# Nine of sixteen B products of a selective scan made by ScalarE on turned data and turned back by TensorE

## The reference

```python
xc = silu(conv(x @ in_w_x) + conv_b)            # 128 inner channels, T = 16384 tokens
dt, B, C = split(xc @ x_w.T)                    # 4, 16 and 16 wide
dt = softplus(dt @ dt_w.T + dt_b)
h_s[t] = exp(dt[t] * A_s) * h_s[t-1] + (dt[t] * xc[t]) * B_s[t]     # for 16 states s
y[t] = sum_s h_s[t] * C_s[t] + xc[t] * D
out = (y * silu(z)) @ out_w.T                   # and once more with time reversed
```

## Time and profile before

| | before |
|---|---|
| time, three runs | 2965.06 us median (2964.64 to 2966.75) |
| the profiled execution | 2967.89 us, span 2966.1 us |
| TensorE busy | 2497.7 us, 84% of the span |
| VectorE busy | 2318.3 us, 78% |
| GpSimd busy | 2084.2 us, 70% |
| ScalarE busy | 1576.8 us, 53% |
| mean granted TensorE clock | 0.90 of full |
| first scan forward to last scan backward | 851 to 2682 us |

### The profile page before, as it was taken

The page is one execution under the profiler, slowest core; times in us unless marked ns, Lnnn a source line. Parts: engine busy times, 40 slices in busy tenths (PEclk is TensorE's granted clock), DMA queues, the critical chain, the costliest instruction groups (busy, mean ns, idle before and its releaser), DMA issues. The chain is left out here.

```text
span 2966.1 us, 34800 instructions
## 1 busy us (share of the span) xinstructions
PE 2497.7 (84%) x7800; PEld 1190.2 (40%) x7800; DVE 2318.3 (78%) x2487; ACT 1576.8 (53%) x2784; POOL 2084.2 (70%) x1166
## 2 busy tenths in 40 slices
PE   7899999957468988889889858899889889988598
PEld 7666666624322323323323223333333333336422
DVE  4366666560659999999999939998999899895499
ACT  6466666543655655555656446555555555545221
POOL 3133333230359999999999949999999999995155
PEclk6699999969779999999999889999999999997599
DMA  3000000000256777777777637776766676660022
GB/s 60 8 9 9 9 9 9 6 1 0 59 167 223 243 244 237 247 235 240 246 236 241 227 124 235 219 236 216 229 226 222 221 225 224 218 211 17 13 54 47
DMA packets 177295, 437.72 MB, mean 148 GB/s; under 512 B 65638, under 2 KB 70219, under 8 KB 177228
## 3 DMA queue, kind: packets, MB, share of 16 engines
q1 hardware_dynamic: 139340, 420.19, 44.5%
q10 hardware_dynamic: 37888, 16.79, 2.1%
HBM read 404.40 MB, written 24.12 MB: 144 GB/s over the span
## 5 line engine op out<-in xcount | busy, mean ns | idle before, releaser
L1443 POOL TENSOR_TENSOR sb_hc<-sb_h,sb_cc 128x1024 f32<-128x1024 f32 x256 | 599.7, 2360 | 61.8 <-PE sb_py L1232 56.2
L1443 POOL TENSOR_TENSOR sf_hc<-sf_h,sf_cc 128x1024 f32<-128x1024 f32 x256 | 595.8, 2347 | 11.5 <-DVE sf_h L1521 8.2
L1232 PE MATMUL sf_py<-sf_hc,ident 128*128 128x512 f32 x1024 | 533.1, 655 | 0.6 <-POOL sf_hc L1443 0.6
L1232 PE MATMUL sb_py<-sb_hc,ident 128*128 128x512 f32 x1024 | 519.5, 638 | 0.0
L572 POOL TENSOR_TENSOR ar_sc<-ar_sc,ar_mx 128x512 f32<-128x512 f32 x128 | 154.7, 1208 | 356.6 <-DVE ar_mx L513 356.6
L1521 DVE TENSOR_TENSOR_SCAN sf_h<-sf_dA,sf_state,sf_pu 128x1024 f32<-128x1024 f32 x160 | 375.4, 2346 | 19.1
L1521 DVE TENSOR_TENSOR_SCAN sb_h<-sb_dA,sb_state,sb_pu 128x1024 f32<-128x1024 f32 x160 | 375.2, 2345 | 17.1
L1232 PEld LDWEIGHTS sf_py<-sf_hc,ident 128*128 128x128 f32 x1024 | 197.0, 205 | 269.3 <-issue 239.8
L1232 PEld LDWEIGHTS sb_py<-sb_hc,ident 128*128 128x128 f32 x1024 | 187.3, 196 | 241.0 <-issue 232.0
L1501 DVE TENSOR_TENSOR sb_pu<-sb_pu,sb_dtx 128x1024 f32<-128x1024 f32 x160 | 193.9, 1212 | 52.7 <-PE sb_pu L1212 52.7
L1436 POOL TENSOR_TENSOR sb_dbx<-sb_dtx,sb_bb 128x1024 f32<-128x1024 f32 x96 | 226.5, 2359 | 3.3 <-DVE sb_dtx L1482 3.3
(11 more groups left out here) (294 smaller groups left out, 4594.6 us busy)
## 6 DMA issues: line engine op xcount, KB each, us to landing
sf_cc<-rows_scratch SPq DMA_DIRECT2D x256, 512.0 KB, 4.4
sb_cc<-rows_scratch SPq DMA_DIRECT2D x256, 512.0 KB, 4.4
sf_bb<-rows_scratch SPq DMA_DIRECT2D x96, 512.0 KB, 5.4
sb_bb<-rows_scratch SPq DMA_DIRECT2D x96, 512.0 KB, 5.4
sf_n<-n_scratch SPq DMA_DIRECT2D x32, 258.0 KB, 5.4
sb_n<-n_scratch SPq DMA_DIRECT2D x32, 258.0 KB, 5.3
y_scratch<-sf_yo SPq DMA_DIRECT2D x16, 512.0 KB, 6.1
sb_yf<-y_scratch SPq DMA_DIRECT2D x16, 512.0 KB, 5.1
```

Source lines behind the costliest of these rows:

```text
L1232: ins = nc.tensor.matmul(p_y[:, hf], lhsT=c.ident[:, :], rhs=hc[:, s % RING, hf], start=False, stop=(s == U - 1))
L1443: nc.gpsimd.tensor_tensor(hc[:, s % RING, :], h[:, s % RING, :], cc[:, s % C_RING, :], ALU.mult).then_inc(read, 1)
```

## The change

`BY_V` shrinks from ten to four states and `BY_G` from six to three. The nine states of the new `BY_A` have their B product made with tokens on the partitions. For that, once per chunk, TensorE makes the B columns with tokens on the partitions (`columns_b`: eight products of 128 tokens x 16 states) and turns dt*x in eight blocks of 128x128 (`turn_x`); ScalarE copies both to SBUF (`take_columns_b`, `take_turned_x`). For each state of `BY_A`, ScalarE multiplies the eight blocks by the state's B column, which is a per-partition scale of an activation (`scale`, three units ahead, ring `sT` of two), and TensorE turns the eight blocks back into `p_u[s % 2]` (`turn_in`, one unit ahead, where `spread_b` stood). The decays of all thirteen states of `BY_V` and `BY_A` (`BY_D`) go to the ring `dA`.

State columns are kept two at a time: in units with odd s, at the end of the unit, the pair (s-3, s-2). The scan of an even state s waits for the pair (s-4, s-3), which is copied in ScalarE's unit s-1. The ring `bb` becomes one buffer, `store_parts` moves from unit 11 to 12 and `load_parts` from 12 to 14. State 0 is now one of GpSimd's.

```diff
-C_RING, B_RING, DECAY_RING = 4, 3, 5
-DECAY_AHEAD, INJECT_AHEAD, LAG_SUM = 3, 2, 4
-BY_G = (2, 5, 7, 10, 13, 15)
-BY_V = tuple(s for s in range(16) if s not in BY_G)
+C_RING, B_RING, DECAY_RING, TURN_RING = 4, 3, 5, 2
+DECAY_AHEAD, INJECT_AHEAD, SCALE_AHEAD, LAG_SUM = 3, 2, 3, 4
+BY_V = (1, 5, 8, 14)
+BY_A = (2, 3, 4, 7, 9, 10, 12, 13, 15)
+BY_D = tuple(sorted(BY_V + BY_A))
+BY_G = tuple(s for s in range(STATES) if s not in BY_D)
...
-        bb, dbx = sb("bb", [128, B_RING, TC]), sb("dbx", [128, B_RING, TC])
+        bb, dbx = sb("bb", [128, TC]), sb("dbx", [128, B_RING, TC])
...
+            def columns_b(m, par):
+                pe.wait_ge(r_copied, m + 1)
+                for j in range(BLOCKS):
+                    ins = nc.tensor.matmul(p_p[:, j * STATES:(j + 1) * STATES], lhsT=xc[:, par, j * Q:(j + 1) * Q],
+                                           rhs=k["bc"][:, 0:STATES], start=True, stop=True)
+                ins.then_inc(bt_made, 1)
+            def turn_x(m, par):
+                pe.wait_ge(dtx_done, m + 1)
+                for j in range(BLOCKS):
+                    ins = nc.tensor.transpose(p_p[:, j * Q:(j + 1) * Q], dtx[:, par, j * Q:(j + 1) * Q], c.ident[:, :])
+                ins.then_inc(x_turned, 1)
+            def turn_in(n, par, s):
+                r = BY_A.index(s)
+                pe.wait_ge(scaled, n * NA + r + 1)
+                need(pe, scanned, n * U + s - 1)
+                for j in range(BLOCKS):
+                    ins = nc.tensor.transpose(p_u[s % 2][:, j * Q:(j + 1) * Q], sT[:, (par * NA + r) % TURN_RING, j, :], c.ident[:, :])
+                ins.then_inc(turned_in, 1)
...
             def project(m, par, last):
                 pe.wait_ge(y_gated, m + 1)
-                pe.wait_ge(dt_done, NC if last else m + 3)
-                pe.wait_ge(dtx_done, NC if last else m + 3)
+                pe.wait_ge(xt_taken, NC if last else m + 3)
...
             prepare = [(0, convolve(a)), (0, convolve(b)), (2, in_out(a)), (3, in_out(b)),
-                       (5, step_size(a)), (6, step_size(b))]
+                       (4, columns_b), (6, step_size(a)), (6, step_size(b)), (13, turn_x)]
             if back:
-                run(pe, unit, prepare, [(13, project)], [(4, gate_in(a)), (4, gate_in(b))])
+                run(pe, unit, prepare, [(14, project)], [(5, gate_in(a)), (5, gate_in(b))])
...
+            def scale(n, par, s):
+                r = BY_A.index(s)
+                if r == 0:
+                    act.wait_ge(bt_taken, n + 1)
+                    act.wait_ge(xt_taken, n + 1)
+                need(act, turned_in, n * NA + r + 1 - TURN_RING)
+                for j in range(BLOCKS):
+                    ins = nc.scalar.activation(sT[:, (par * NA + r) % TURN_RING, j, :], dtxT[:, j, :], ACT.Copy,
+                                               scale=bT[:, par, j, s:s + 1])
+                ins.then_inc(scaled, 1)
...
             def keep(n, s):
-                act.wait_ge(scanned, n * U + s + 1)
+                act.wait_ge(scanned, n * U + s + 2)
                 e = 0 if back else TC - 1
-                nc.scalar.copy(state[:, s:s + 1], h[:, s % RING, e:e + 1]).then_inc(kept, 1)
+                nc.scalar.copy(state[:, s:s + 2], h[:, s % RING:s % RING + 2, e]).then_inc(kept, 1)
...
                 m, mpar, ms = after(n, par, s + DECAY_AHEAD)
-                if ms in BY_V and not (last and s + DECAY_AHEAD >= U):
+                if ms in BY_D and not (last and s + DECAY_AHEAD >= U):
                     decay_v(m, mpar, ms)
-                if s >= 2:
-                    keep(n, s - 2)
-                elif not first:
-                    keep(n - 1, s - 2 + U)
+                m, mpar, ms = after(n, par, s + SCALE_AHEAD)
+                if ms in BY_A and not (last and s + SCALE_AHEAD >= U):
+                    scale(m, mpar, ms)
+                if s % 2 and s >= 3:
+                    keep(n, s - 3)
+                elif s % 2 and not first:
+                    keep(n - 1, s - 3 + U)
...
-            prepare = [(1, silu_x), (4, bc_rows), (5, load_flat), (6, part_high), (7, softplus_relu), (7, softplus_abs),
-                       (8, softplus_exp), (8, softplus_one), (8, softplus_log), (9, part_middle), (11, store_parts),
-                       (11, take_dt), (12, load_parts)]
+            prepare = [(1, silu_x), (4, bc_rows), (5, load_flat), (5, take_columns_b), (6, part_high), (7, softplus_relu),
+                       (7, softplus_abs), (8, softplus_exp), (8, softplus_one), (8, softplus_log), (9, part_middle),
+                       (11, take_dt), (12, store_parts), (14, take_turned_x), (14, load_parts)]
...
-                run(act, unit, prepare, [(1, silu_z)], [(1, exp_log_tables), (5, take_z)])
+                run(act, unit, prepare, [(1, silu_z)], [(1, exp_log_tables), (6, take_z)])
...
-                need(dve, kept, u + 1 - RING)
+                if s % 2 == 0:
+                    need(dve, kept, n * PAIRS + (s - RING) // 2 + 1)
...
-                [(LAG_SUM - 1, gate), (14, add_x)] if back else [])
+                [(LAG_SUM - 1, gate), (15, add_x)] if back else [])
...
-                need(sp, g_injected, n * NG_ + r + 1 - B_RING)
-                spread_row(bb[:, r % B_RING, :], n, s, b_spread[r % B_RING])
+                need(sp, g_injected, n * NG_ + r)
+                spread_row(bb[:, :], n, s, b_spread)
```

More of the change, by code:

```diff
@@ L939 @@
 FLAT = STATES * TC // 128
+BLOCKS = TC // Q
 def state_space_stage(nc, c, W, y_scratch, rows, nd, split):
@@ L1072, in scan_direction @@
     U = STATES
-    NV, NG_ = len(BY_V), len(BY_G)
+    NV, NG_, NA, ND = len(BY_V), len(BY_G), len(BY_A), len(BY_D)
+    PAIRS = U // 2
     with ExitStack() as ctx:
@@ L1092, in scan_direction @@
         yo = sb("yo", [128, TC])
+        bT, dtxT = sb("bT", [128, 2, BLOCKS, STATES]), sb("dtxT", [128, BLOCKS, INNER])
+        sT = sb("sT", [128, TURN_RING, BLOCKS, INNER])
         if back:
@@ L1111, in scan_direction @@
             sem(s) for s in ("r_copied", "r_stored", "f_loaded", "high", "remained", "middle", "lowest", "p_stored"))
+        bt_made, bt_taken, x_turned, xt_taken, scaled, turned_in = (
+            sem(s) for s in ("bt_made", "bt_taken", "x_turned", "xt_taken", "scaled", "turned_in"))
         p_loaded = [sem("p_loaded%d" % j) for j in range(2)]
@@ L1114, in scan_direction @@
         c_spread = [sem("c_spread%d" % j) for j in range(C_RING)]
-        b_spread = [sem("b_spread%d" % j) for j in range(B_RING)]
+        b_spread = sem("b_spread")
         block = ctx.enter_context(nc.Block())
@@ L1127, in past @@
         def past(order, n, s, ring):
-            r = order.index(s) - ring
-            return n * U + order[r] + 1 if r >= 0 else (n - 1) * U + order[r + len(order)] + 1
+            r = order.index(s)
+            if r >= ring:
+                return n * U + order[r - ring] + 1
+            return (n - 1) * U + order[max(q for q in range(len(order)) if q % ring == r % ring)] + 1
         def run(eng, unit, prepare=(), tail=(), own=()):
@@ L1162, in step @@
                 def step(m, par, last):
-                    pe.wait_ge(r_copied, NC if last else m + 2)
+                    pe.wait_ge(bt_taken, NC if last else m + 2)
                     if last:
-                        pe.wait_ge(dt_done, NC)
-                        pe.wait_ge(dtx_done, NC)
+                        pe.wait_ge(xt_taken, NC)
                     ins = nc.tensor.matmul(p_p[:, hf], lhsT=k["z"][:, :],
@@ L1175, in step @@
                     pe.wait_ge(n_loaded[par], 16 * (m + 2 - par))
-                    need(pe, dt_done, m)
-                    need(pe, dtx_done, m)
+                    need(pe, xt_taken, m)
                     if back:
@@ L1189, in step @@
                 def step(m, par):
-                    pe.wait_ge(r_copied, m + 1)
+                    pe.wait_ge(bt_taken, m + 1)
                     if back:
@@ L1255, in unit @@
                     spread_b(m, mpar, ms)
+                if ms in BY_A and not (last and s == U - 1):
+                    turn_in(m, mpar, ms)
                 if s >= LAG_SUM:
@@ L1319, in take_dt @@
                 act.wait_ge(dt_summed, m + 1)
-                need(act, v_decayed, NV * (m - 1))
+                need(act, v_decayed, ND * (m - 1))
                 need(act, g_decayed, NG_ * (m - 1))
@@ L1329, in bc_rows, with take_columns_b, take_turned_x @@
                 nc.scalar.dma_start(rows[bass.ds(m, 1), :, :].rearrange("a r t -> (a r) t"), brow[:, :]).then_inc(r_stored, 16)
+            def take_columns_b(m, par):
+                act.wait_ge(bt_made, m + 1)
+                nc.scalar.copy(bT[:, par, :, :].rearrange("p j s -> p (j s)"), p_p[:, 0:BLOCKS * STATES]).then_inc(bt_taken, 1)
+            def take_turned_x(m, par):
+                act.wait_ge(x_turned, m + 1)
+                need(act, scaled, NA * m)
+                nc.scalar.copy(dtxT[:, :, :].rearrange("p j d -> p (j d)"), p_p[:, :]).then_inc(xt_taken, 1)
```

(29 more changed lines are left out.)

4 lines of the change are left out of this document (2 added, 2 removed).

## The result

The kernel with the change takes 3112.03 us median (3108.47 to 3118.13, four runs) against 2964.85 for the kernel before on the same chip: a ratio of 1.0505, 95% interval 1.0478 to 1.0532. Slower, as predicted, but by 147 us instead of 79. The profiled execution spans 3110.2 us against 2966.1 before, 144.1 more.

A forecast was written before the change was run, and what follows sets the result against it. Before, GpSimd bounds forward; with the change ScalarE was to set 59.0 us forward against 53.9 and 58.5 backward against 57.9. +76, +9, -6 each for last chunks, +3 each for first: +79 on 2966, 3045 us; range 2915 to 3160.

The forecast's parts named there:

- The scaling's price: ScalarE's 128x128 scalings by a B column pointer, 72 a chunk: 0.295 us each, 21.3 us a chunk.
- (1): Rival: ScalarE's scaling is cheap, 1.3 to 1.6 us a state; 2873 us, or up to 2900; chance 0.16.
- (3): Rival: a state's eight scalings on ScalarE don't overlap, 6.6 us more a chunk, 3250 us; chance 0.12.
- The four 512-column activations: Upper bound for the scaling on ScalarE: four take 2.37 us without overlap, so a scaling would be 0.39.
- ScalarE's sum: ScalarE's work per chunk adds up to 54.1 us before waits; over 50 us busy was the sign.
- the stall ahead of scan 0: VectorE loses 2.4 us, as state copies 12 and 13 come after 4.7 us and scan 15 covers 2.3.
- The DMA waits on ScalarE's path: Forward, ScalarE waits 1.0 us for the rows' store (landing 3.6) and 1.2 for the flat load (4.9).
- The rest of the forward sum: ScalarE's forward path from scan 14's end to keeping pair 8, 9: 48.9 us; with its tail 59.0.
- Which tail ends the chunk: Forward after pair 8, 9: VectorE's tail 9.4 us gives 58.3, ScalarE's 10.1 with the parts' store gives 59.0, taken.
- unit 4: TensorE's long backward unit, over 7 us, claimed hidden because scan 6 waits longer for ScalarE's pair 2, 3.
- rival (4): TensorE's clock falls to 0.85; backward 5 us more a chunk, 3120 us; chance 0.07.
- Rival (2): Waits vanish because ScalarE runs ahead elsewhere: 54.3 us forward, 55.2 backward, 2925 us; chance 0.12.

The follow-up runs named there:

- flat_later: The changed kernel with the flat load of the B rows and the first part issued later in ScalarE's program: 3069.8 us, ratio 1.0367 to before.
- half_turn: The changed kernel with only four of each state's eight blocks turned back, all eight still scaled (incomplete result): 3097.7 us, ratio 1.0458 to before.
- front_light: The changed kernel with single state copies and later flat load, minus seven of eight B column products and the backward D term: 3000.8 us, ratio 1.0138.
- six_thirteen: The changed kernel with six scaled states instead of nine, thirteen decays kept, single state copies and a later flat load: 3047.6 us, ratio 1.0284.
- both_half: The changed kernel with four of each state's eight blocks scaled and four turned back (incomplete result): 2968.4 us, ratio 1.0010 to before.

## Why the prediction was right or wrong

**The scaling's price: right.** 0.295 was taken, 0.304 measured. It was read from the exp with a pointer and lay between the copy's 0.16 and the full 0.39. Rivals (1) and (3) fall with it. The four 512-column activations that don't overlap were no guide for this form.

**ScalarE's sum and the stall ahead of scan 0: right.** It was to be over 50 us busy and is at 52.3 and 53.1. Before scan 0, VectorE was to lose 2.4 us:

```profile
1334.73 4.58 DVE L1586 TENSOR_TENSOR_SCAN sf_h<-sf_dA,sf_state,sf_pu 128x1024 f32<-128x1024 f32 x2
1342.01 2.35 DVE L1586 TENSOR_TENSOR_SCAN sf_h<-sf_pu,sf_state,sf_dbx 128x1024 f32<-128x1024 f32 x1 [2.70 <-ACT sf_state L1426]
```

It is 2.70 in this chunk (start, duration; in brackets the idle time and its releaser), and 39.7 us in 15 chunks. GpSimd at 0.78 of the chunk was foreseen too.

**The DMA waits on ScalarE's path: the term that was mis-sized.** Rows' store and flat load were put at 1.0 and 1.2 us. In a chunk of after, on ScalarE (ACTq is its queue issuing a DMA):

```profile
1360.67 0.98 ACT L1360 COPY sf_brow<-sf_pp 32x1024 f32<-32x1024 f32 x1
1361.82 0.36 ACTq L1362 DMA_DIRECT2D rows_scratch<-sf_brow  x1
...
1364.39 0.18 ACT L1426 COPY sf_state<-sf_h 128x2 f32<-128x2 f32 x1
1368.10 0.38 ACTq L1388 DMA_DIRECT2D sf_flat<-rows_scratch  x1
1368.53 0.27 ACT L1366 COPY sf_bT<-sf_pp 128x128 f32<-128x128 f32 x1 [3.96 <-DMA rows_scratch<-sf_brow]
```

ScalarE stands 3.96 us for the store, 3.2 in the mean. It has the size and the bytes of before, but lands later:

```profile
rows_scratch<-sf_brow ACTq DMA_DIRECT2D x16, 128.0 KB, 5.6
...
sf_flat<-rows_scratch ACTq DMA_DIRECT2D x16, 64.0 KB, 2.7
```

5.6 us against 3.6, and the flat load 2.7 against 4.9. I took a landing time of before as a constant. The store's wait costs 2.2 us a chunk more than I gave it, the flat load 1.0 less. The loads of the B rows, put at 5 us each at most, land 3.9 to 6.5 us after their issue forward, 4.8 in the median, but no product of GpSimd waits for one. flat_later shows that this wait is worth its full size forward: 3.2 us of it went and the period fell by 3.2.

**The rest of the forward sum.** Worked through the chunk whose zero (end of scan 14) is at 1337.05: the pairs are kept at 18.2 (0, 1), 27.3, 39.4, 48.2 and 53.9 us (8, 9); by the prediction's terms at 16.4, 24.5, 34.5, 43.2 and 48.9. So the path came out 5.0 us long in this chunk, of 63.7 in all. The mean chunk is 61.1, 2.1 over the 59.0 forecast: 2.2 - 1.0 from the two DMAs, 0.7 from the scalings (72 x 0.009), some 0.4 from single scalings that start 1.8 us late with no releaser in the trace (6.7 us in all of the direction), 0.75 from waits around y and its copy. The sum of these is 3.0, and as one tail fell away (next) they stand on a base of 58.3, so 61.3 of 61.1.

**Which tail ends the chunk: wrong.** I took ScalarE's, 59.0, because load_parts would wait for the store of the parts, 5.4 us. There is no such wait. The trace of ScalarE at the end of a chunk:

```profile
1389.94 1.14 ACT L1414 ACTIVATE sf_dA<-sf_dt,ss_A 128x1024 f32<-128x1024 f32 x1
1390.20 0.41 ACTq L1402 DMA_DIRECT2D split_scratch<-sf_parts  x1
...
1393.02 2.44 ACT L1380 ACTIVATE sf_sT<-sf_dtxT,sf_bT 128x128 f32<-128x128 f32 x8
...
1397.89 0.35 ACTq L1408 DMA_DIRECT2D sf_bcs<-split_scratch  x1
```

The store is issued at 1390.20, although in the program it stands behind the decay and the scaling that run from 1391.97 and 1393.02 to 1395.46. It lands in 1.9 us in the median, long before load_parts at 1397.89. Before, ScalarE did stand for this store, 47.4 us in 15 times; that wait was carried over. VectorE's tail is the one that counts, 9.4 predicted and 9.3 found. VectorE even sets the pace from scan 10 on: scan 10 waited for the pair 6, 7 in 15 chunks (45.4 us), scan 12 for the pair 8, 9 in one only. By the prediction's terms both ways round are equally long: 43.2 us for the pair 6, 7 and 15.25 for five scans and three passes of 1.2, 58.4 against 58.3. The right number then was 58.3 and not 59.0, by chance on the side that made my error smaller.

**Backward: the period near, the reason wrong.** 58.5 was forecast with ScalarE as its bound: scan 6 would wait for the pair 2, 3, and that would hide TensorE's unit 4. It is 60.2. Scan 6 never waited for a state copy there, and scan 7 waited for its turned block in every chunk, 3.9 us in the mean and in the row at 2077.36; before, VectorE had stood up to 3.4 us for a B row behind the same unit. So unit 4 was not hidden, and TensorE is on the path (half_turn, front_light). That the period came within 1.7 us is luck as far as its reason goes. In the trace of after:

```profile
2085.64 1.04 PE L1235 MATMUL sb_pu<-ident,sb_sT 128*128 128x128 f32 x8
2086.51 3.60 PE L1264 MATMUL sb_py<-sb_hc,ident 128*128 128x512 f32 x8
2092.37 1.19 PE L1235 MATMUL sb_pu<-ident,sb_sT 128*128 128x128 f32 x8 [2.26 <-DVE sb_h L1586]
2093.35 3.52 PE L1264 MATMUL sb_py<-sb_hc,ident 128*128 128x512 f32 x4
2096.71 1.04 PE L1235 MATMUL sb_pu<-ident,sb_sT 128*128 128x128 f32 x8
```

TensorE runs from 2042.17 with one gap of 0.73 to 2090.11, waits 2.26 us for a scan, and then the product of one state takes 3.52 for four instructions, where the eight of an earlier row took 3.60 and four take 1.88 one chunk later (below). The clock says why (stretches; granted clock is third from the end):

```profile
2086.50:2090.10 3.60, 3.60 (x10) 1.34 (x8) 2.01 (x3) 3.60 (x12) 3.60 (x2) 1.00 0.88 249
2093.40:2096.70 3.30, 3.30 (x5) 1.14 (x5) 3.30 (x3) 3.30 (x8) 3.30 (x3) 0.51 0.33 120
```

0.51 after the idle stretch, 1.00 before it. That costs TensorE 1.6 us beside the 2.3 of the wait. It does not come each time. One chunk later, after the same wait:

```profile
2152.87 1.09 PE L1235 MATMUL sb_pu<-ident,sb_sT 128*128 128x128 f32 x8 [2.26 <-DVE sb_h L1586]
2153.80 1.88 PE L1264 MATMUL sb_py<-sb_hc,ident 128*128 128x512 f32 x4
...
2153.90:2157.20 3.30, 2.22 (x9) 0.92 (x8) 3.30 (x3) 3.30 (x8) 3.30 (x3) 1.00 0.37 106
```

The wait, 2.1 to 2.5 us, stands in all 15 chunks from 1912 us on, and the clock fell at it in ten of them: in the 3.3 us that start 1.0 us after it, 0.50 to 0.69 was granted in these ten and 1.00 in the other five. From the third chunk on, the period that follows is 60.3 to 60.5 us where it fell and 60.0 to 60.2 where it didn't: of the 1.6 us about 0.3 reach the period. In the two chunks of the first profile rows behind the result the clock is 0.97 and 1.00 (0.94 and 0.97 before), so rival (4), a clock that sinks through the stage, to an assumed 0.85, did not come: with 80 blocks turned among float32 products a chunk, the granted clock is no lower than before. A stretch of turning alone is in no run here.

Rival (2), ScalarE running ahead, fell: its zero point is scan 14, as argued.

**The whole sum: 79 us forecast, 144.1 in the profiled execution.** The fourteen periods gave 96.0 us forward and 32.7 backward, where 5.1 and 0.6 a period make 71 and 8: 49 of the missing 65 us. The stretch from the first scan to the first dt*x, which I had counted as a fifteenth period, grew by 6.3 and 10.7 us instead of 5.1 and 0.6: another 11. The last chunks gave back 4.4 and 6.0 (6 each forecast), and the preparation ahead of the first scans took 2.7 and 1.8 more (3 each forecast), both near. The last 4.4 us lie behind the last scan, mostly in stages that the change leaves alone. So the two periods, and in them the store's wait forward and TensorE's unit 4 backward, are where the forecast fell short.

What stays open: how the 2.3 us of the backward period split between TensorE and ScalarE, for half_turn took off 1.1 only; why earlier state copies lengthen the backward chunk; what sets 56.3 us forward once ScalarE has six scaled states (the two candidates under six_thirteen); and why the rows' store lands 2 us later than before and the parts' store 3.5 us sooner.

## What to carry to other kernels

An engine at 58% busy is not a free engine. 21 us of new work on it in a 54 us chunk also puts every small thing that others wait for, here a state copy of 0.1 us and a DMA wait, behind a queue that has no slack left; find those small things and their waits first. A DMA's landing time is not a constant of the transfer: where a wait in an engine's program hangs on it, put more work over it than the trace of before says (here 5.6 us were needed where 3.6 had been read). And where two engines are close, as at 59 and 60 us backward here, an edit to one alone shows little more than the gap to the other (half_turn 1.1 us, both_half 2.0).

## What the runs showed that was not expected

A DMA on ScalarE's queue can leave before compute that the program puts ahead of it (1390.20 against the scaling that ran until 1395.46). A wait on a DMA can thus be shorter than program order lets one think. Scalings of 128 columns with a pointer overlap by 0.08 us each (388 lasting, 304 apart), where the four activations of rows 8 overlapped by nothing. After some 2.3 us of idling in the backward direction TensorE's granted clock fell, to 0.50 to 0.69 over the next few us, in ten chunks of 15 and stayed at 1.00 in five, with the same program around it.
